# Two feed-forward layers on one core: FP4 rounding of two units in one set of VectorE operations, with the way down four to five units behind

## The reference, cut to what matters

```
x = x + 0.5 * ffn(layernorm(x))            # twice: before and after the attention
def fp4_linear(x, w): return fp4(x) @ fp4(w).T
ffn(x): gate = fp4_linear(x, w_gate); y = fp4_linear(x, w_up)     # 128 -> 352 each
        h = silu(gate) * y
        return fp4_linear(h, w_down)                              # 352 -> 128
fp4(v): per block of 16 values: scale = max(max|v| / 6, 1e-12); v / scale is put
        on the grid 0, .5, 1, 1.5, 2, 3, 4, 6 (with sign), and multiplied by scale
```

## Time and profile before

| | us |
|---|---|
| median of three runs | 2018.29 (2016.92 to 2018.34) |
| the profiled execution: its time | 2015.0 |
| its span, first to last instruction | 2013.3 |
| first feed-forward layer | 22.6 to 196.8 of the span |
| second feed-forward layer | 1038.2 to 1212.6 of the span |

### The profile page before, as it was taken

One profiled execution on the slowest core, in us unless ns is written; L12 is line 12 of the kernel. 1 busy time (PEld: TensorE's weight loads), 2 busy tenths in 40 slices (PEclk: granted clock), 3 DMA queues, 4 the chain that ended last, 5 costly groups with the idle time before them and its releaser, 6 DMA issues. The chain is left out here.

```text
span 2013.3 us, 32025 instructions
## 1 busy us (share of the span) xinstructions
PE 1543.9 (77%) x10355; PEld 869.9 (43%) x10355; DVE 1468.0 (73%) x3104; ACT 885.3 (44%) x2173; POOL 1012.1 (50%) x1324
## 2 busy tenths in 40 slices
PE   2466799999999999999956564079468888851696
PEld 1344233333333333333324344057257767741473
DVE  7989677777777777777757997168577777772484
ACT  1321454444444444444413322057157766620472
POOL 1321266656565656566632324747345555637473
PEclk9888699999999999999977895589779999965798
DMA  6000000000000000000000000233300000002235
GB/s 205 0 0 0 5 23 22 22 22 22 22 22 22 22 22 22 22 22 22 22 16 0 0 1 30 72 87 103 102 1 1 1 2 1 1 20 72 81 105 159
DMA packets 90179, 70.51 MB, mean 35 GB/s; under 512 B 16608, under 2 KB 84640, under 8 KB 90016
## 3 DMA queue, kind: packets, MB, share of 16 engines
q1 hardware_dynamic: 81312, 49.57, 9.1%
q0 software_dynamic: 8704, 18.89, 2.7%
HBM read 29.32 MB, written 22.30 MB: 26 GB/s over the span
## 5 line engine op out<-in xcount | busy, mean ns | idle before, releaser
L662 DVE TENSOR_REDUCE at_nmax<-at_score 128x1 f32<-128x512 f32 x512 | 329.2, 685 | 139.4 <-PE at_score L789 139.4
L753 ACT ACTIVATE at_pT<-at_turned 128x512 f32<-128x512 f32 x512 | 277.9, 595 | 343.0 <-PE at_turned L817 343.0
L648 POOL TENSOR_TENSOR m_rows<-m_rows,at_pT 128x512 f32<-128x512 f32 x256 | 319.4, 1268 | 95.0 <-ACT at_pT L753 95.0
L648 POOL TENSOR_TENSOR m_rows<-at_pT 128x512 f32<-128x512 f32 x128 | 160.2, 1271 | 250.2 <-ACT at_pT L753 250.2
L865 PE MATMUL at_pv<-at_pT,at_v 128*64 128x512 f32 x1024 | 261.7, 611 | 0.4 <-DVE at_oT L692 0.4
L1056 POOL DMA_INDIRECT by_token<-m_ysb,m_dest x144 | 137.8, 957 | 88.0 <-DVE m_ysb L1136 53.9
L1050 POOL DMA_INDIRECT by_expert<-m_rows,m_slot x128 | 123.1, 962 | 70.8 <-issue 38.4
L377 POOL TENSOR_TENSOR f_hq<-f_hg,f_hsc 128x704 f32<-128x704 f32 x32 | 44.3, 1385 | 168.2 <-DVEq L348 168.2
L115 DVE TENSOR_SCALAR la_xn<-la_y,la_ln_mean,la_ln_rstd 128x128 f32<-128x128 f32 x192 | 81.7, 485 | 52.6 <-POOLq L1478 52.6
L450 PE MATMUL f_gate<-m_wguT,f_xqT 128*128 128x352 f32 x128 | 63.9, 588 | 73.1 <-DVEq L343 71.8
L685 DVE RECIPROCAL m_rows<-m_rows 128x256 f32<-128x256 f32 x64 | 111.6, 1743 | 2.9 <-ACT m_rows L759 2.9
(11 more groups left out here) (311 smaller groups left out, 3662.7 us busy)
## 6 DMA issues: line engine op xcount, KB each, us to landing
m_rows<-m_rows SPq DMA_DIRECT2D x512, 32.0 KB, 1.8
m_xin<-by_expert SPq DMA_DIRECT2D x144, 72.0 KB
m_rows<-by_token SPq DMA_DIRECT2D x32, 256.0 KB, 4.6
by_token<-m_ysb,m_dest POOLq DMA_INDIRECT x144, 2.3
m_x<-in_x SPq DMA_DIRECT2D x8, 256.0 KB, 4.8
by_expert<-m_rows,m_slot POOLq DMA_INDIRECT x128, 2.3
out_x<-m_x SPq DMA_DIRECT2D x8, 256.0 KB, 4.1
by_expert<-m_pad SPq DMA_DIRECT2D x18, 72.0 KB, 1.6
```

The costliest lines, as they stand in the source:

```text
L648: done = nc.gpsimd.tensor_tensor(acc, before, pT[g % 2][:, head, kt, :], ALU.add)
L662: nc.vector.tensor_reduce(nmax[:, head * DH + qt:head * DH + qt + 1], score[head][:], AX.X, ALU.max, negate=True)\
L753: nc.scalar.activation(pT[g % 2][:, head, kt, :], turned[head][:], ACT.Exp).then_inc(exp_done, 1)
```

## The change

The rounding is cut in two: `fp4_ratio` (block maximum, scale, reciprocal, ratio) and `fp4_round` (mask, constant, addition, subtraction). Units 0 to 13 are rounded in seven pairs, on 1408 elements per partition. Pair m-1 gets its ratio between the `h` of units 2m and 2m+1, and its rounding after the `h` of unit 2m+1. `h`, `hg` and `hsc` hold two units each, twice over. Units 14 and 15 are rounded alone. TensorE turns `hq` of unit n-4 and multiplies unit n-5 in its step n, in two functions, five steps running past the last unit. Additions lie five units back. `x_part(1)` moves to between the first two `h`; `x_part(2)` and `x_part(3)` come right behind the rounding of units 2 and 3, and of units 6 and 7. The turn of x and ScalarE's share of the layer norm move from the second unit of a group to the third and fourth.

```diff
--- before.py
+++ after.py
@@ -121,23 +121,32 @@
-def fp4_grid(nc, ch, src, q, scale, w):
+def fp4_ratio(nc, ch, src, scale, w):
+    amax, rs, y = w["amax"][:, 0:nb], w["rscale"][:, 0:nb], w["ratio"][:, 0:n]
+    ch.link(nc.vector.tensor_tensor(blk(y), blk(src), rs.unsqueeze(2).to_broadcast([P, nb, BLK]), ALU.mult))
+def fp4_round(nc, ch, q, w):
+    n = q.shape[1]
+    y, m = w["ratio"][:, 0:n], w["magic"][:, 0:n]
     ch.link(nc.vector.tensor_tensor(q, y, m, ALU.subtract))
+def fp4_grid(nc, ch, src, q, scale, w):
+    fp4_ratio(nc, ch, src, scale, w)
+    fp4_round(nc, ch, q, w)
...
+    LAG = 5
...
+        TWO = 2 * UT * INTER
+        w = {"amax": s.sb("amax", [P, TWO // BLK]), "rscale": s.sb("rscale", [P, TWO // BLK]),
+             "ratio": s.sb("ratio", [P, TWO]), "magic": s.sb("magic", [P, TWO])}
...
+        silu = s.sb("silu", [P, UT, INTER])
+        h = [s.sb(f"h{i}", [P, 2, UT, INTER]) for i in range(2)]
+        hg = [s.sb(f"hg{i}", [P, 2, UT * INTER]) for i in range(2)]
+        hsc = [s.sb(f"hsc{i}", [P, 2, UT * INTER // BLK]) for i in range(2)]
...
+                def hidden(n):
+
+                    dve.wait_ge(silu_done, n + 1)
+                    ch.link(nc.vector.tensor_tensor(h[n // 2 % 2][:, n % 2], silu[:], up[:, :, 0:INTER], ALU.mult))
+                    nc.vector.sem_inc(h_done, 1)
+
+                def pair_ratio(m):
+
+                    if m >= 2:
+                        dve.wait_ge(hq_done, 2 * m - 2)
+                    fp4_ratio(nc, ch, h[m % 2][:].rearrange("p a t i -> p (a t i)"), hsc[m % 2][:].rearrange("p a b -> p (a b)"), w)
+
+                def pair_round(m):
+
+                    fp4_round(nc, ch, hg[m % 2][:].rearrange("p a i -> p (a i)"), w)
+                    nc.vector.sem_inc(hg_done, 2)
+
+                def alone(n):
+
+                    i, k = n // 2 % 2, n % 2
+                    dve.wait_ge(hq_done, 2 * (n // 2) - 2)
+                    fp4_grid(nc, ch, h[i][:, k].rearrange("p t i -> p (t i)"), hg[i][:, k, :], hsc[i][:, k, :], w)
+                    nc.vector.sem_inc(hg_done, 1)
...
-                for g in range(GROUPS):
-                    for v in range(UPG):
-                        n = g * UPG + v
-                        i = v % 2
-                        dve.wait_ge(silu_done, n + 1)
-                        ch.link(nc.vector.tensor_tensor(h[:], silu[:], up[:, :, 0:INTER], ALU.mult))
-                        nc.vector.sem_inc(h_done, 1)
-                        if n >= 2:
-                            add(n - 1)
-                            dve.wait_ge(hq_done, n - 1)
-                        fp4_grid(nc, ch, h[:].rearrange("p t i -> p (t i)"), hg[i][:], hsc[i][:], w)
-                        nc.vector.sem_inc(hg_done, 1)
-                        if v == 0 and g + 1 < GROUPS:
-                            x_part(g + 1, ch)
+                for m in range(UNITS // 2):
+                    g = 2 * m // UPG
+                    hidden(2 * m)
+                    if 2 * m > LAG:
+                        add(2 * m - LAG)
+                    if m:
+                        pair_ratio(m - 1)
+                    else:
+                        x_part(1, ch)
+                    hidden(2 * m + 1)
+                    if 2 * m + 1 > LAG:
+                        add(2 * m + 1 - LAG)
+                    if m:
+                        pair_round(m - 1)
+                    if m and 2 * m % UPG == 0 and g + 1 < GROUPS:
+                        x_part(g + 1, ch)
+                alone(UNITS - 2)
+                add(UNITS - 5)
+                add(UNITS - 4)
+                alone(UNITS - 1)
+                add(UNITS - 3)
+                add(UNITS - 2)
+                dve.wait_ge(added, UNITS - 2)
+                for t in range(NT - 2 * UT):
+                    nc.vector.bn_stats(mem["x_stats"][:, t, :], mem["x"][:, t, :])
                 add(UNITS - 1)
                 dve.wait_ge(added, UNITS - 1)
-                for t in range(NT - UT):
+                for t in range(NT - 2 * UT, NT - UT):
                     nc.vector.bn_stats(mem["x_stats"][:, t, :], mem["x"][:, t, :])
                 add(UNITS)
...
                 x_part(0)
+                x_part(1)
                 for n in range(UNITS):
                     i = n % 2
+                    if n and n % UPG == 0 and n // UPG + 1 < GROUPS:
+                        x_part(n // UPG + 1)
                     pool.wait_ge(hg_done, n + 1)
                     if n >= 2:
                         pool.wait_ge(h_turned, n - 1)
...
-                    if n % UPG == 0 and n + UPG < UNITS:
-                        x_part(n // UPG + 1)
...
                     if n + 1 < UNITS:
                         act.wait_ge(h_done, n + 1)
                         silu_gate(n + 1)
-                    if n:
-                        h_out(n - 1)
+                    if n >= LAG - 1:
+                        h_out(n - LAG + 1)
                     g, v = divmod(n, UPG)
-                    if v == 1 and g + 1 < GROUPS:
+                    if v == 2 and g + 1 < GROUPS:
                         x_out(g + 1, (g + 1) % 2)
-                    if v and g + 2 < GROUPS:
-                        if v == 1:
+                    if v >= 2 and g + 2 < GROUPS:
+                        if v == 2:
                             act.wait_ge(xg_done, g + 2)
-                        norm(g + 2, 6 * v - 6, min(6 * v, 2 * GT))
+                        norm(g + 2, GT * (v - 2), GT * (v - 1))
...
-                h_out(UNITS - 1)
+                for n in range(UNITS - LAG + 1, UNITS):
+                    h_out(n)
...
-                def way_down(n):
+                def turn_hidden(n):
 
                     i = n % 2
                     pe.wait_ge(hq_done, n + 1)
...
                     last.then_inc(h_turned, 1)
+
+                def way_down(n):
+
                     pe.wait_ge(hqT_ready, n + 1)
                     if n:
                         pe.wait_ge(added, n)
...
                 gate_up(0, 0)
-                for n in range(UNITS):
+                for n in range(UNITS + LAG):
                     g, v = divmod(n, UPG)
                     if n + 1 < UNITS:
                         pe.wait_ge(h_done, n + 1)
                         if v == UPG - 1:
                             pe.wait_ge(xqT_ready, 2 * g + 4)
                         gate_up((v + 1) % UPG, (n + 1) // UPG % 2)
-                    if n:
-                        way_down(n - 1)
-                    if v == 1 and g + 1 < GROUPS:
+                    if n >= LAG:
+                        way_down(n - LAG)
+                    if 0 <= n - LAG + 1 < UNITS:
+                        turn_hidden(n - LAG + 1)
+                    if v == 2 and g + 1 < GROUPS:
                         turn(g + 1)
-                way_down(UNITS - 1)
```

More of the change, by code:

```diff
@@ L280, in ffn_stage @@
         xqT = [s.sb(f"xqT{i}", [P, GT * P]) for i in range(2)]
-        silu, h = (s.sb(n, [P, UT, INTER]) for n in ("silu", "h"))
-        hg = [s.sb(f"hg{i}", [P, UT * INTER]) for i in range(2)]
-        hsc = [s.sb(f"hsc{i}", [P, UT * INTER // BLK]) for i in range(2)]
+        silu = s.sb("silu", [P, UT, INTER])
+        h = [s.sb(f"h{i}", [P, 2, UT, INTER]) for i in range(2)]
+        hg = [s.sb(f"hg{i}", [P, 2, UT * INTER]) for i in range(2)]
+        hsc = [s.sb(f"hsc{i}", [P, 2, UT * INTER // BLK]) for i in range(2)]
         hq = [s.sb(f"hq{i}", [P, UT, INTER_PAD]) for i in range(2)]
@@ L479, in way_down @@
                         for j in range(3):
-                            last = nc.tensor.matmul(down[:, t * P:(t + 1) * P], hqT[i][:, t, j * P:(j + 1) * P],
+                            last = nc.tensor.matmul(down[:, t * P:(t + 1) * P], hqT[n % 2][:, t, j * P:(j + 1) * P],
                                                     mem["wdT"][:, j * P:(j + 1) * P], start=(j == 0), stop=(j == 2))
```

10 lines of the change are left out of this document (2 added, 8 removed).

## The result

The changed kernel takes 2030.84 us (median of 4 runs, 2029.61 to 2031.88) where the kernel before takes 2018.32 (4 runs, 2016.92 to 2020.25): a ratio of 1.0065, 95% interval 1.0051 to 1.0078. It is slower, by 12.5 us; forecast were 17.6. The profiled execution took 2031.3 us, span 2029.1.

The account below looks back on a forecast made before the run. VectorE was taken to set the pace, busy 152.8 of 174.2 us and 153.4 of 174.4. The terms -22.4 - 11.5 + 0.3 + 11.2 + 8 + 13.2 + 18.8 gave +17.6 us: 2036 us from the median 2018.3, range 2024 to 2044.

Parts of the forecast that it names:

- eight operations instead of sixteen, with the statistics' extra stop: VectorE's rounding, seven pairs in two layers: wider operations save 22.4 us, a third stop for statistics adds 0.3.
- waits for the way down that go: VectorE's additions inside the layers no longer wait for their product, with small waits gone too: -11.5 us, bounds -8 and -12.
- the opening: Between `h` of units 1 and 2 VectorE has no pair to work on: 5.6 us a layer, +11.2 us.
- silu late after a rounding of x: After `x_part(2)` and `x_part(3)` `h` waits for the silu, 2.0 us each, four times: +8 us.
- the end of a layer: Last additions wait for products through the one bank `down`: 3.0, 2.3 and 1.8 us, less 0.5 before; +13.2 us.
- the shared port: VectorE's locking operations stall until GpSimd's queued rescalings and subtractions finish: 26.9 us less 8.1 before, +18.8 us.
- The 58 cycles: Fixed term per VectorE operation, 60 ns, from the Trainium skill; a pair would save 0.75 us, the sum 12 us higher.
- I am wrong if the scale keeps its 0.2 us: Sign for the port stalls: VectorE's scale should average near 1 us instead of 0.2, with maxima near 4.
- one GpSimd operation at a time: Rival: VectorE gets the lock when GpSimd's running operation ends; -8 us against the forecast, 2028 us, chance 0.15.
- VectorE is not held: Rival: GpSimd's queued operations let the scale through at once, all 26.9 us of stalls go; 2009 us, chance 0.09.
- a colder TensorE: Rival: TensorE stays at 1.2 GHz through a layer, every ratio half waits 1.2 us; 2049 us, chance 0.12.

Follow-up runs that it names:

- early: Changed kernel with each pair's ratio behind its own second `h`, rounding behind the next, additions four units back instead of five: 2009.64 us, ratio 0.9964 to the kernel before.
- two_banks: Changed kernel with products 11, 13 and 15 in a second PSUM bank, the one the turns of x no longer use: 2012.05 us, ratio 0.9977 to the kernel before.
- the probe: Test stage before the first layer: GpSimd starts three memsets or multiplications, VectorE asks during the first; its small operation takes about 0.40 us behind memsets, 1.17 behind multiplications.
- no_wait: early with four `hq` buffers and one `h`, GpSimd waiting only at a pair's first unit, not before its second rescaling: 2085.08 us, ratio 0.9965 to the kernel before.

## Why the prediction was right, and where it was not

The forecast's sum was +17.6 us, the layers grew by 12.3. By its own steps:

| step | forecast | measured |
|---|---|---|
| eight operations instead of sixteen, with the statistics' extra stop | -22.1 | -22.8 |
| waits for the way down that go | -11.5 | -10.6 |
| the opening | +11.2 | +14.8 |
| silu late after a rounding of x | +8 | +9.0 |
| the end of a layer | +13.2 | +15.5 |
| the shared port | +18.8 | +6.4 |
| sum | +17.6 | +12.3 |

The first row is what is left of the difference in length when idle time and stalls are taken off (12.3 - 28.7 - 6.4); the second is what is left of the idle time; the others are read off the rows above. The end is 16.4 less the 0.94 of before.

- **Width was priced rightly.** The price per element and the fixed part, both from pairs of shapes in the trace of before, gave 1.626 us for an operation on 1408 elements; it takes 1.625. VectorE's busy time without stalls falls by 8.6 and 8.9 us a layer, where I had 9. The 58 cycles that I had set beside it stand in the table of the Trainium skill, "VectorE: DVE Perf Modes", section on the TRN2 errata; the text below that table puts the measured fixed term at about 150 cycles. At the 0.96 GHz of the same table that is, as an estimate, 156 ns, and the 160 of the earlier trace rows agree with it. By the 58 cycles the row would lie 12 us higher than it does.
- **The waits stand where they were forecast**: one at the opening, one after each of the first `h` behind x, three at the end, none elsewhere. Only sizes are off. The opening was 5.6 a layer and is 7.3 and 7.5, above the upper bound of 6.8: two or three further `h` are late, and I had one of them, in the upper bound only. My sum for the slow case was wrong too: 1.0 + 5.16 + 0.8 is 7.0, not 6.7, so 6.0 us of waiting, and the profiles have 5.82 and 5.11, and 6.06 twice in the second one. Behind x 9.0 is near 8 by luck in part, as the layers have 3 and 6. At the end the second product was to cost 2.3; it cost 3.08, since the product that VectorE held back for 3.50 us ran at a granted clock of 0.50. early and two_banks show both as causes, not only as rows: with work in the gap the opening's wait falls to 1.73 us, and with a second bank the waits at the end fall to 0.57. (early also has one product less behind the last gate and up, which is 5.9 of its 18.6 us of idle time.)
- **The step that failed is the shared port.** I let the first locking operation of VectorE stand until GpSimd's whole queue was done, 26.9 us in all. It stands to the end of the one operation that runs, and then the two take turns. By my own sign, "I am wrong if the scale keeps its 0.2 us", this step was wrong: 19 of the 26 scales of the layers keep it, and the longest takes 1.30 us, where I had maxima near 4. The rival "one GpSimd operation at a time" had the mechanism and 0.15; its own sum, -8 us, was still too small, since this term came out 12.4 lower. Its 2028 us lie 3 from the measured 2031, the forecast's 2036 lie 5 from it: the rival with 0.15 was nearer in mechanism and in time than the forecast with 0.60. I gave it little because of the earlier trace rows, one place with another kind of GpSimd instruction, which the probe doesn't bear out., with the kind that this change queues, show one operation and no more.
- **The time fell into the range partly because errors cancel**: 12.4 us too much for the port, 7 too little for opening, x and end together. With these three as forecast and the port as measured the sum would be 5.2, which is 2023.5 us and just under the range's 2024. The rivals "VectorE is not held" and "a colder TensorE" did not come about: the stalls are real, and TensorE was granted 0.88 and 0.77 of its clock in the layers, against 0.87 and 0.78, with 2.4 and 1.5 us more of busy time.

What stays open: why VectorE stood through two memsets at the earlier trace rows, and why the waits behind x are twice as long in the second layer. A kernel without GpSimd's weight slices, or with its rescalings at another engine, was not tried.

## What to carry to other kernels

A lag buys freedom in the middle of a loop and is paid for where the loop ends: count how many results are still to come through one buffer after the last input, and give that stretch its second bank, before anything else is weighed. When work is grouped in pairs, look for the first pair and for the step after each interruption, for there the engine that groups has nothing to do while the others make its input; here half of the grouped work could be put there. And price two engines that share a port as these rows show them, taking turns instruction by instruction, with the remainder of the running instruction as the cost of each meeting (the earlier trace rows is the one place that does not fit), and look at both engines, for either can be the one that is held.

## What was not expected of the hardware

- In the probe VectorE's small operation ended 0.03 us behind the end of the running GpSimd operation in every round (1.17 us against 1.26, 0.12 after its start), and no queued GpSimd operation went ahead of it. GpSimd in turn stood behind VectorE: 2.36 us for a rescaling of 1.385.
- A `tensor_scalar` on few elements can slip in between two GpSimd operations and cost neither of them more than 0.05 us: 0.20 us at 1107.39 above, and again at 120.32 in no_wait.
- The kernel before takes 2018 us on one chip and 2092 and 2099 on two others; in the profiles the difference stands behind the second layer, in the part that is not touched. The changed kernel's ratio was 1.0065 on one and 1.0058 on another, inside each other's intervals.
